# Strassen units: one more of them, PSUM sums seeded by ScalarE, and relation 0's two edge tables added by VectorE

## What is computed

```python
def _rgcn(x, edge_index, edge_type, weight, root, bias):
    src, dst = (edge_index[0], edge_index[1])
    msgs = x[src]
    out = x @ root + bias
    for r in range(weight.shape[0]):              # 8 relations, weight[r] is 1024 x 1024
        mask = (edge_type == r)
        sums = segment_sum(msgs * mask[:, None], dst, num_segments=n)
        cnt = segment_sum(mask, dst, num_segments=n)
        out = out + (sums / maximum(cnt, 1.0)[:, None]) @ weight[r]
    return out
```

## Time and profile before

| | |
|---|---|
| median of 3 runs | 1109.83 us (1107.57 to 1111.14) |
| the profiled execution, its own time | 1113.76 us |
| its span | 1112.0 us |
| its mean granted clock | 0.982 of full speed |

### The profile page before, as it was taken

How to read it: one execution, slowest core, us unless ns; L and a number is a source line. 1 busy time by engine, 2 the same in 40 slices (tenths; PEclk the granted TensorE clock), 3 DMA queues, 4 the chain that set the end, 5 groups by cost and what they waited for, 6 DMA issues and landing times.

```text
span 1112.0 us, 14475 instructions
## 1 busy us (share of the span) xinstructions
PE 1066.2 (96%) x5385; PEld 891.4 (80%) x5385; DVE 793.0 (71%) x1591; ACT 413.9 (37%) x647; POOL 417.4 (38%) x272
## 2 busy tenths in 40 slices
PE   6998999999999999999999998999979999999995
PEld 5776887777787777889999998887756878888774
DVE  7567888889989897317667776495479648876647
ACT  3331333434434343122332323361443415256652
POOL 6023488788788888212442330000010000410016
PEclk9999999999999999999999999999989999989998
DMA  9999978788977776799999742523242201588757
GB/s 322 400 331 383 327 181 145 193 218 208 223 193 147 196 140 161 169 244 219 271 261 252 170 126 99 208 83 126 60 80 89 76 2 59 223 281 277 235 180 258
DMA packets 94475, 217.34 MB, mean 195 GB/s; under 512 B 29978, under 2 KB 46173, under 8 KB 85947
## 3 DMA queue, kind: packets, MB, share of 16 engines
q1 hardware_dynamic: 39488, 137.19, 36.5%
q0 software_dynamic: 37504, 48.18, 21.8%
q10 hardware_dynamic: 17406, 30.97, 10.1%
HBM read 149.59 MB, written 66.71 MB: 195 GB/s over the span
## 4 chain that ended last, share of the span: by engine, by line
PE 78%; DVE 10%; DMA 6%; ACT 3%; issue 1%; ACTq 1%; POOLq 0%; SPq 0%; DVEq 0%
PE ps L583 65%; PE ps L891 3%; PE ps L928 3%; DVE rl L414 3%; DVE EQ L1578 3%; DMA stage<-in_w_e 2%; PE ps L855 2%; DMA stage<-in_w_rel 2%; DMA KR<-key_scratch 2%; PE ps L573 1%; ACT rh L405 1%; DVE V L1498 1%; ACT He L1106 1%; PE ps L939 1%; PE ps L906 1%
## 5 line engine op out<-in xcount | busy, mean ns | idle before, releaser
L2219 POOL DMA_INDIRECT adj_scratch<-cnt,idx x164 | 288.9, 1762 | 133.8 <-issue 43.6
L414 DVE TENSOR_TENSOR rl<-stage,rh 128x512 fp32r<-128x512 f32 (+1 forms) x264 | 213.4, 837 | 152.3 <-ACT rh L405 148.7
L405 ACT CAST rh<-stage 128x512 fp32r<-128x512 f32 (+1 forms) x264 | 180.4, 716 | 364.9 <-PE ps L583 242.8
L583 PE MATMUL ps<-rh,xTh 128*125 128x512 f32 x600 | 239.0, 398 | 5.7 <-ACT He L1106 4.6
L583 PE MATMUL ps<-rl,xTh 128*125 128x512 f32 x600 | 237.5, 396 | 0.0
L583 PE MATMUL ps<-rh,xTl 128*125 128x512 f32 x600 | 237.4, 396 | 0.0
L583 PE MATMUL ps<-rh,Ar 125*125 125x342 f32 x600 | 190.8, 323 | 5.4 <-issue 4.0
L583 PE MATMUL ps<-rl,Ar 125*125 125x342 f32 x600 | 190.3, 322 | 0.0
L583 PEld LDWEIGHTS ps<-rh,xTh 128*125 128x125 f32 x600 | 112.0, 187 | 35.9 <-ACT He L1106 7.2
L583 PEld LDWEIGHTS ps<-rh,xTl 128*125 128x125 f32 x600 | 112.1, 187 | 28.4
L583 PEld LDWEIGHTS ps<-rl,xTh 128*125 128x125 f32 x600 | 112.0, 187 | 27.4
(11 more groups left out here) (295 smaller groups left out, 1615.1 us busy)
## 6 DMA issues: line engine op xcount, KB each, us to landing
stage<-in_w_rel SPq DMA_DIRECT2D x22, 1024.0 KB, 6.4
stage<-h_scratch SPq DMA_DIRECT2D x24, 855.0 KB, 7.3
stage<-in_w_e SPq DMA_DIRECT2D x16, 1024.0 KB, 6.6
adj_scratch<-Z POOLq DMA_DIRECT2D x16, 767.0 KB, 20.1
adj_scratch<-Z SPq DMA_DIRECT2D x16, 767.0 KB, 16.1
h_scratch<-He ACTq DMA_DIRECT2D x40, 257.0 KB, 9.1
h_scratch<-He ACTq DMA_DIRECT2D x40, 256.0 KB, 4.7
KR<-key_scratch ACTq DMA_DIRECT2D x37, 256.0 KB, 6.5
```

The lines of the kernel that those rows point to most:

```text
L405: e.copy(h, s).then_inc(*a_hi.up(*[("hi", t) for t in step(i)]))
L414: e.tensor_tensor(l, s, h.bitcast(F32), ALU.subtract).then_inc(*v_lo.up(*[("lo", t) for t in step(i)]))
L583: ins = e.matmul(ps[0:P, b, 0:width], a, m, start=first and n == 0, stop=last and n == len(parts) - 1, skip_group_check=again)
L2219: e.indirect_dma_start(accd[to], bass.IndirectOffsetOnAxis(ap=idx[:, n:n + 1], axis=0), cnt[:, n:n + 1], None, compute_op=ALU.add).then_in ...
```

## The change

- `FAST` gets unit 3, and the S matrices are made in the two halves of unit 2, (1, 0) and (1, 1).
- The sums X, Z and E2 no longer begin at zero: ScalarE first copies another sum from PSUM to PSUM (`seed`), X from W, Z from -X, E2 from -E1, and TensorE accumulates on top of it.
- With that VectorE's operations on X and Y (V2, V3) and its last three output tiles become ScalarE's copies, and V5 is gone. `fast_before` keeps the tiles after t1 and t4.
- Key windows: five a fast unit, three in each half of unit 2, none in unit 3 otherwise.
- Relation 0: GpSimd loads both tables, into `acr[0]` and `acr[1]`. VectorE adds them into the operand, after the tiles of the root unit's second half. GpSimd then loads relation 1's first table into `acr[1]`, and the second on top. `adjacency_copy(0)` is gone; `adjacency_copy(1)` stands where it stood.

```diff
-WINDOWS = {(0, 1): (0, 2, 4, 6), (1, 0): (0, 1, 2, 4, 5, 6), (1, 1): (0, 2, 4), (2, 0): (2, 4, 6), (2, 1): (0, 2, 4, 6),
+WINDOWS = {(0, 1): (0, 2, 4, 6), (1, 0): (0, 2, 4), (1, 1): (0, 2, 4),
-FAST = (4, 5, 6, 7, 8)
+FAST = (3, 4, 5, 6, 7, 8)
+SEEDED = (("X", 0), ("X", 1), ("Z", 0), ("Z", 1), ("E", 2))
-KEYS_IN_FAST = {u: (3, 10, 17, 24) for u in FAST}
-S_IN = ((1, 1), (2, 0))
+KEYS_IN_FAST = {u: (2, 8, 13, 18, 24) for u in FAST}
+S_IN = ((1, 0), (1, 1))
 # TensorE, part() of fast_unit()
                     on.wait_ge(*at("lo", i))
-                    for ev in (*ready, *(old if start else ())):
+                    if start and seeded:
+                        before_seed[u, role] = old
+                        on.wait_ge(*at("seed", u, role))
+                    for ev in (*ready, *(old if start and not seeded else ())):
                         on.wait_ge(*at(*ev))
-                    return three(b, i, stat, start, stop, kind in ("t4", "b21", "b22"))
+                    return three(b, i, stat, start and not seeded, stop, seeded or kind in ("t4", "b21"))
 # ScalarE
+            def seed(u, role, source, sign, ready):
+                to, b = (ps[0:P, banks.of["fast", u, *name], :] for name in (role, source))
+                on.wait_ge(*at(*ready))
+                for ev in before_seed[u, role]:
+                    on.wait_ge(*at(*ev))
+                e.activation(to, b, ACT.Copy, scale=sign).then_inc(*a_out.up(("seed", u, role)))
 # fast_between(i)
                     if i - F0[u] == 13:
                         for p in range(2):
+                            seed(u, ("X", p), ("W", p), 1.0, ("fast", u, "b11", ("W", p)))
+                    if i - F0[u] == 17:
+                        for p in range(2):
+                            on.wait_ge(*at("fast", u, "t2", ("X", p)))
...
+                            e.copy(V2[0:P, p, :], ps[0:P, banks.of["fast", u, "X", p], :]).then_inc(*a_out.up(("v2", u, p)))
+                            seed(u, ("Z", p), ("X", p), -1.0, ("fast", u, "t2", ("X", p)))
+                        seed(u, ("E", 2), ("E", 1), -1.0, ("fast", u, "b11", ("E", 1)))
+                    if i - F0[u] == 21:
+                        for p in range(2):
...
+                            e.copy(V3[0:P, p, :], ps[0:P, banks.of["fast", u, "Y", p], :]).then_inc(*a_out.up(("v3", u, p)))
...
-                    if i - F0[u] == 39:
+                    if i - F0[u] == (36 if u == FAST[-1] else 37):
+                        for p in range(2):
+                            h_copy(u, 2 * p, 1, banks.of["fast", u, "Z", p], "fast", u, "b22", ("Z", p))
+                        h_copy(u, 4, 1, banks.of["fast", u, "E", 2], "fast", u, "b22", ("E", 2))
                         for c in (0, 2, 4):
                             h_store(u, c, 1)
 # ScalarE, the loop over the units
-                    if unit == 0 and hf == 1:
-                        adjacency_copy(0)
 # VectorE, the loop over the units
+                    if unit == 0 and hf == 1:
+                        for i in range(2):
+                            on.wait_ge(*at("adj part", i))
+                        on.wait_ge(*at("slot zero"))
+                        on.wait_ge(*at("fast", FAST[-1], "b22", ("E", 2)))
+                        e.tensor_tensor(ar_flat(0), acb[0], acb[1], ALU.add).then_inc(*v_row.up(("adj", 0)))
 # GpSimd
-            for r in range(2):
+            for i in range(2):
                 on.wait_ge(*at("added", NG - 2))
                 on.wait_ge(*at("added", NG - 1))
...
-                e.dma_start(acr[r], adjacency(r, 0)).then_inc(*d_adj_first[r].up(("acb first", r)))
-            for r in range(2):
-                second_adder(r)
+                e.dma_start(acr[i], adjacency(0, i)).then_inc(*d_adj_first[i].up(("adj part", i)))
+            on.wait_ge(*at("adj", 0))
+            e.dma_start(acr[1], adjacency(1, 0)).then_inc(*d_adj_first[1].up(("acb first", 1)))
+            second_adder(1)
```

More of the change, by code:

```diff
@@ L224, in gnn_ffn_kernel @@
         He = sb("He", [128, NHE, 514], F32, ph0)
-        V5 = sb("V5", [128, 512], F32, phx)
-        phx.close()
         er = [sb(f"er{i}", [128, 2, 128], I32, ph0) for i in range(3)]
@@ L312, in gnn_ffn_kernel @@
         banks = Banks()
+        before_seed = {}
         groups, tiles, tile, vacant, latest = [], [], {}, [], {}
@@ L645, in part @@
                     b, old = held[role]
+                    seeded = role in SEEDED
                     on.wait_ge(*at("lo", i))
-                    for ev in (*ready, *(old if start else ())):
+                    if start and seeded:
+                        before_seed[u, role] = old
+                        on.wait_ge(*at("seed", u, role))
+                    for ev in (*ready, *(old if start and not seeded else ())):
                         on.wait_ge(*at(*ev))
-                    return three(b, i, stat, start, stop, kind in ("t4", "b21", "b22"))
+                    return three(b, i, stat, start and not seeded, stop, seeded or kind in ("t4", "b21"))
                 def ends(ins, kind, j, role, last_role):
@@ L660, in fast_unit @@
                 for p in range(2):
-                    held["X", p] = banks.take(("fast", u, "X", p), ("v2", u, p), where=of.get(("X", p)))
+                    held["X", p] = banks.take(("fast", u, "X", p), ("v2", u, p), ("seed", u, ("Z", p)), where=of.get(("X", p)))
                 for p in range(2):
@@ L686, in fast_unit @@
                     for p in range(2):
-                        ends(part("b21", j, ("W", p), x_stat(4 + j, 2 * p), False, j == 3, ("v1", u, p)), "b21", j, ("W", p), ("E", 1))
-                    ends(part("b21", j, ("E", 1), x_stat(4 + j, 4), False, j == 3, ("v5", u)), "b21", j, ("E", 1), ("E", 1))
+                        ends(part("b21", j, ("W", p), x_stat(4 + j, 2 * p), False, j == 3, ("seed", u, ("X", p))), "b21", j, ("W", p), ("E", 1))
+                    ends(part("b21", j, ("E", 1), x_stat(4 + j, 4), False, j == 3, ("seed", u, ("E", 2))), "b21", j, ("E", 1), ("E", 1))
                 for j in range(4):
@@ L1111, in fast_between @@
                         for p in range(2):
-                            on.wait_ge(*at("fast", u, "b11", ("W", p)))
+                            seed(u, ("X", p), ("W", p), 1.0, ("fast", u, "b11", ("W", p)))
+                    if i - F0[u] == 17:
+                        for p in range(2):
+                            on.wait_ge(*at("fast", u, "t2", ("X", p)))
                             on.wait_ge(*at("s lo", 3, 1))
                             if u != FAST[0]:
[L1115 to L1121, removed]
+                                on.wait_ge(*at("he", u - 1, 2 * p + 1, 0))
+                            e.copy(V2[0:P, p, :], ps[0:P, banks.of["fast", u, "X", p], :]).then_inc(*a_out.up(("v2", u, p)))
[3 more added lines that the diff above has]
+                        for p in range(2):
+                            on.wait_ge(*at("fast", u, "t3", ("Y", p)))
+                            on.wait_ge(*at("s lo", 1, 1))
+                            if u != FAST[0]:
+                                on.wait_ge(*at("he", u - 1, 2 * p + 1, 1))
+                            e.copy(V3[0:P, p, :], ps[0:P, banks.of["fast", u, "Y", p], :]).then_inc(*a_out.up(("v3", u, p)))
                     if i - F0[u] == 27:
@@ L1181, in adjacency_copy @@
                 on.wait_ge(*at("acb", r))
-                if r == 0:
-                    on.wait_ge(*at("slot zero"))
-                    on.wait_ge(*at("fast", FAST[-1], "b22", ("E", 2)))
                 if r == 1:
@@ L1437, in fast_before @@
                 for u in FAST:
[L1438 to L1450, removed]
                     if i - F0[u] == 25:
@@ L1456, in fast_before @@
                             h_made(u, 2 * p + 1, 0, banks.of["fast", u, "Y", p], V2[0:P, p, :], ALU.add, ("fast", u, "t4", ("Y", p)), ("v2", u, p))
[L1457 to L1460, removed]
             def fast_after(i):
@@ L2237, in total @@
                     e.tensor_tensor(flat, flat, arf, ALU.add).then_inc(*p_row.up(("total", r)))
-            for r in range(2):
+            for i in range(2):
                 on.wait_ge(*at("added", NG - 2))
                 on.wait_ge(*at("added", NG - 1))
-                for c in (0, 2, 4):
-                    on.wait_ge(*at("he", FAST[-1], c, 1))
+                for c in (1, 3):
+                    on.wait_ge(*at("he", FAST[-1], c, 0))
                 for j in range(4):
                     on.wait_ge(*at("lo", tile["fast", FAST[-1], "b22", j]))
-                e.dma_start(acr[r], adjacency(r, 0)).then_inc(*d_adj_first[r].up(("acb first", r)))
-            for r in range(2):
-                second_adder(r)
+                e.dma_start(acr[i], adjacency(0, i)).then_inc(*d_adj_first[i].up(("adj part", i)))
+            on.wait_ge(*at("adj", 0))
+            e.dma_start(acr[1], adjacency(1, 0)).then_inc(*d_adj_first[1].up(("acb first", 1)))
+            second_adder(1)
```

## The result

The changed kernel takes 1138.1 us (median of 4 runs, 1136.6 to 1142.19), the kernel before in the same comparison 1109.88: a ratio of 1.0258, 95% interval 1.0231 to 1.0285, so 28 us slower. The forecast was 1143, in a range of 1120 to 1154, for two delays. The profiled execution took 1136.6 us (span 1134.9). The two spans differ by 22.9 us only: the execution profiled before was 3.9 us over its median, this one 1.5 under.

A forecast was written before the change was run, and what follows sets the result against it. TensorE, busy 96% of the 1112.0 us span, was taken as the bound. Delays of 14.5 us (first fast unit) and 18.6 us (relation 1) sum to 33.1, giving 1143 us on the median's basis, range 1120 to 1154.

The forecast's parts named there:

- Removed work and steady seeds: Unit 3 drops from 240 to 216 matmuls, 5.4 us less; seeds of X in steady units cost 0.
- First fast unit: Unit 3: TensorE stands before t2 for late weights, VectorE, then ScalarE; +14.5 us, with the 5.4 saved included.
- VectorE's chain: Before unit 3's t2: sums, key windows, low parts and S operations from b22's landing to the last S matrix, 21.9 us.
- ScalarE's series: Before unit 3's seed of X: five copies of unit 2's second half, after the last S matrix's cast, 5.65 us.
- Relation 1: Spread of relation 0: relation 1's late table copy stands ahead of the cast of h(0,1) in ScalarE's list; +18.6 us.
- R: The end of the root unit, 499.5 in the trace before; the prediction's reference time for table loads and copies.
- the meeting with GpSimd: Low parts of h(0,1) take 7.51 us, not 1.94, beside GpSimd's addition of relation 1; VectorE first would give 1138.
- Sum: Whole kernel: 14.5 + 18.6 = 33.1 us slower, 1147 on the profiled execution's basis, 1143 on the median's.
- relation 1 in time: Rival at the spread: relation 1's table arrives in time, leaving only the first delay, 1124 us; chance 0.11.
- a free ScalarE: Rival, faster: a held ScalarE costs TensorE nothing because ten tiles are prepared, 1102 us; chance 0.08.
- weights early: Rival at unit 3: its weights pass the zero fills or these are done, +1.3 + 18.6, 1130 us; chance 0.13.
- late seeds: Rival in every fast unit: seeds come late, 1.5 us a unit, +9, 1152 us; chance 0.09.

The follow-up runs named there:

- experiment 7: Against the kernel before: only units 4 to 8 seeded, with ScalarE's copies; unit 3 plain, S matrices, key windows and table pair as before; 1109.91 us, 1.0001.
- experiment 9: Changed kernel with paired tables, S matrices half a unit earlier, fourth zero fills behind b22/b21, ScalarE's copies earlier, unit 2's four second-half key windows moved; 1100.52 us.
- experiment 4: Changed kernel with ScalarE's five copies of unit 2's second half two tiles earlier in its list; 1133.12 us, 1.0213 to the kernel before.
- experiment 5: Changed kernel with the fourth group of zero fills issued behind unit 3's b22 and b21 loads; 1134.56 us, 1.0214 to the kernel before.
- experiment 6: Changed kernel with S matrices half a unit earlier and four key windows in unit 2's second half; 1131.2 us, 1.0195 to the kernel before.
- experiment 10: Changed kernel without ScalarE's seed of X in unit 3, so W's part is missing there; 1132.66 us, 1.0194 to the kernel before.
- experiment 1: Changed kernel with the tables of relations 0 and 1 loaded and accumulated as a pair again, ScalarE copying both; 1120.53 us, 1.0088 to the kernel before.
- experiment 2: Changed kernel with only ScalarE's copy of relation 1 moved behind the casts of h(0,1) and h(0,2); 1125.56 us, 1.0169 to the kernel before.
- experiment 3: Changed kernel with GpSimd's addition of relation 1 waiting until VectorE's low parts of h(0,1) are made; 1132.34 us, 1.0217 to the kernel before.

## Why the prediction was right, step by step

- **Removed work and steady seeds**: priced at -5.4 and 0. Units 4 to 8 take 50.04 to 50.10 us, and experiment 7 finds no change. The margin of 1 us at the seed of X was about right: in unit 5 ScalarE is idle 1.16 us ahead of the last cast before the seed, and a window more near the end of the unit before uses the margin up (experiment 9).
- **First fast unit**: +14.5 forecast, 9.4 found in the traces. VectorE's chain (21.9) and ScalarE's series (5.65) came as worked out. The term that was off is b22's landing, 129.5 instead of 134.2. It was issued at 103.06, 19 us earlier than the row I took, and landed 4.7 earlier: most of the earlier issue was lost in the queue, as assumed, but not all. Why the landing came 4.7 us earlier was not tried (three key windows fewer load their keys before it). Experiments 4 and 5 show the links to be in series; none alone removes the stop, experiment 6 included. One hold the prediction left out: X's bank is freed by the first of the same five copies, so t2 would have waited for ScalarE without any seed (experiment 10), and the seed alone is not the price.
- **Relation 1**: +18.6 forecast, 15.15 found. VectorE's add took 3.41 us (3.4 forecast), the load landed at R + 1.8 (R + 1.4), the accumulating load took 11.45 us and not 14, the copy 2.80, and the meeting with GpSimd recurred, 6.05 us for the low parts. Experiments 1, 2 and 3 show the order of the tables as the cause: with the copy moved in ScalarE's list 4.08 us of the stop stay, with the pair of tables none, and the meeting is 4.1 us of the 15.1. GpSimd's addition had begun first, and VectorE's low parts ended at 532.50, 1.80 us after it (530.70), about the 1.94 that they take alone. For such a meeting the Trainium skill, page "SBUF — State Buffer", section "Who interferes with whom", says that the order of issue decides who blocks. The trace agrees for GpSimd first; no run here lets VectorE go first into a table operation of GpSimd, since experiment 3 only keeps the two apart (1.94 us).
- **Sum**: 33.1 forecast for the profiled execution, 22.9 between the two profiles, 28.2 between the medians. The bases of the two profiled executions differ by more than I allowed: 5.4 us, not 3.9 (0.35%). Of the 10.2 us by which the traces miss the forecast, 5.1 are the first delay, 3.45 the second and 1.6 the shorter rest. So both delays came as worked out, each smaller, and that the medians differ by only 4.9 us less than forecast, where the traces differ by 10.2 less, is partly luck of the spread between executions. It is luck, too, that it falls on the 1138 given for VectorE going first in the meeting: GpSimd went first.
- **Rivals**: relation 1 in time and a free ScalarE are refuted by the two stops; weights early is true in part, since 4.7 of the 13.2 us between the two cases (seed at 164.6 or 151.4) were gone, and VectorE still waited 5.01 us for b22; late seeds by units 4 to 8.

## What to carry to other kernels

An engine that runs a list in order makes every wait in it a wait of all that stands behind: before moving work onto it, ask of each waiting entry what is queued behind, and put copies that free banks, and casts that feed TensorE, ahead of entries that wait for another engine. The lead of ten tiles hid such waits here in the units that follow one another alike, and not at the first fast unit and the first spread; the first stage of a new kind is the place to check. And when a bound is lifted, the next is near: here VectorE's windows, then relation 0's table behind GpSimd's adds.

## What was not expected of the hardware

In experiment 2 the low parts of h(0,1) began on VectorE before GpSimd's copy of relation 0's table and still took long; VectorE and GpSimd:

```profile
509.29 5.65 DVE L414 TENSOR_TENSOR rl<-stage,rh 125x1710 fp32r<-125x1710 f32 x1 [1.04 <-ACT rh L405]
```

```profile
509.67 3.46 POOL L2240 COPY Atot<-Ar 128x3125 f32<-128x3125 f32 x1
```
